# Layer-2 cross-attention: the reads of two tiles of keys together in every second step, with four buffers of exponentials

## The chip, the core and the metric

One NeuronCore of a Trainium2 chip runs the whole program, a four-layer block of attention and feed-forward parts in float32. The metric is the device time of one execution in microseconds (us). Three runs of the kernel before gave 1391.83, 1392.6 and 1385.4 us; their median is 1391.83 us.

## The reference, cut to what matters

The change touches one of the twelve parts, the cross-attention of layer 2. It has two batches of 128 queries and 32 heads of width 8. The queries attend to themselves (with a mask), and to a context of 2048 keys; both reads are summed, the second scaled by tanh of a gate for each head.

```python
q, k, v = heads(x @ Wq), heads(x @ Wk), heads(x @ Wv)      # 32 heads of 8
q, k = rope(q), rope(k)
w = softmax(max(q @ k.T * 8**-0.5 + mask, lowest))          # 128 x 128 for a head
out = w @ v
a_k, a_v = heads(context @ Wk), heads(context @ Wv)         # 2048 keys
out = out + tanh(gate) * softmax(q @ a_k.T * 8**-0.5) @ a_v
return out @ Wo
```

## The kernel before, in words

The function layer_L2X (from line 1509) writes out, engine by engine, a program of instructions that wait on semaphores. After a prologue (normalization, projections, rope), a loop runs over 6 stages. A stage is one batch and one of three groups of heads, c: groups 0 and 1 have 12 heads (three in each of four groups of 32 rows), group 2 has 8 (two in each). The order is (0,2), (0,0), (0,1), (1,0), (1,1), (1,2) as (batch, c); so stages 0 and 5 are of two heads and stages 1 to 4 of three. Each stage has 16 steps, one for each tile of 128 keys.

In step t of stage s TensorE issues, in this order:

- second_scores(s, t), line 1719: four matmuls, one for each group g of 32 rows, of keys by queries with the maximum already folded in; the result of each (128 keys by 384 or 256 columns) goes to its own PSUM bank. ScalarE takes the exponential of each bank into the buffer ex (line 1908).
- context_v, line 1651, in some steps: the values of two tiles of keys (in stage 0 at t = 5, in stage 2 at odd t from 3, in stage 3 at t = 1). ScalarE copies them (line 1835).
- first_scores for the next stage, line 1703: sets of four matmuls of 128 queries by 512 keys, each into its own bank, of which VectorE takes the row maximum (line 1996). At t % 4 == 1 there are two sets where the next stage has three heads, one where it has two; at t % 4 == 3 one set. Stage 5 issues none; the last step of a stage issues the first set for the stage after the next.
- self_scores, line 1665, at t % 4 == 3, taken by VectorE (line 1954).
- read(s, t - 1), line 1733: for each head the values of tile t - 1 (128 keys by 32 columns, as weights) times the exponentials, added up over the 16 tiles in one bank, "read". It waits until the exponentials of its tile are there. At t = 0 it is the last tile of the stage before.
- the other sets of first_scores; then self_read (line 1682, t % 4 == 0), context_k (line 1642, t % 4 == 1, stages 0 to 3), self_turn (line 1673, t % 4 == 2), turn_reads (lines 1689 and 1694, t = 2), turn_max (line 1711, t = 14).

All blocks but the read share a ring of seven PSUM banks. The class Turns hands them out in order: a take waits for the semaphore that says that the use seven takes back has been emptied by ScalarE or VectorE. A matmul of float32 is recorded as two instructions (two passes), so that the four matmuls of a block of scores count as x8.

The buffer ex holds the exponentials of NE = 3 tiles. Before the exponentials of step n, ScalarE waits for the read of tile n - NE. All engines work through their own list in order; TensorE's order is written out by hand in the loop.

Of the kernel before, what the change touches and what calls it, by code (L numbers as in the profile page):

```python
# [23 lines left out]
P = 128  # L24
B = 2
D = 256
# [3 lines left out]
NT = S2 // P  # L30
# [1478 lines left out]
def layer_L2X(env):  # L1509
# [5 lines left out]
    L = Layer(env, "L2X")  # L1515
# [3 lines left out]
    TRIO = 3 * P  # L1519
# [3 lines left out]
    ring = [L.bank(f"ring{j}") for j in range(NR)]  # L1523
    bank_o = L.bank("read")
    head = Head(L, ring[2])
    y = L.sb("y", [P, B, D])
    tail = Tail(L, y, ring[0], ring[1], w("Wo"))
    maskt = L.sb("mask", [P, B * TRIO])
    q, k = L.sb("q", [P, B, D]), L.sb("k", [P, B, D])
    tmp = L.sb("rope_tmp", [P, B, D])  # L1530
    kT = L.sb("self_kT", [P, NC, B, P])
    qm = L.sb("q_masked", [P, B, NC, 3, P])
    qx = L.sb("q_and_max", [P, 2, TRIO])
    mxs = L.sb("max_spread", [P, 2, 3, P])
    parts, mx = L.sb("max_parts", [P, 3, NG, 4]), L.sb("max", [P, 3 * NG])
    smx = L.sb("self_max", [P, 3])
    se, spT = L.sb("self_exp", [P, TRIO]), L.sb("self_probsT", [P, TRIO])
    soT = L.sb("self_readT", [P, NG, P])
    NE = 3
    ex = L.sb("context_exp", [P, NE, NG, TRIO])  # L1540
    qp, kp = ex[:, 0, 0:B, :], ex[:, 0, B:2 * B, :]
    cT = L.sb("context_kT", [P, 3, S2])
    cvp = L.sb("context_v_ones", [P, NT, NH * VW + 32 - VW])
    svp = L.sb("self_v_ones", [P, B, NH * VW + 32 - VW])
    cv, sv = (a[:, :, 0:NH * VW].rearrange("p t (h e) -> p t h e", e=VW) for a in (cvp, svp))
    oT = L.sb("readT", [P, TRIO])
    tg, inv, ya = L.sb("tanh_gate", [P, NH]), L.sb("inv_den", [P, 3 * NG]), L.sb("out_part", [P, 3 * NG * HD])
    names = ("dve_chain", "buffers_set", "mask_loaded", "gate_tanh", "qkv_done", "q_roped", "k_roped", "self_v_copied",
             "q_rope_ready", "k_rope_ready", "q_turned", "k_turned", "last_q_masked", "q_masked_ready", "self_kT_copied",
# [11 lines left out]
    NSTG = len(stages)  # L1561
# [3 lines left out]
    def heads(c):  # L1565
        return 2 if c == 2 else 3

    def head_at(c, g, j):
        return 12 * c + heads(c) * g + j

    def width(s):
        return heads(stages[s][1]) * P

    def done(n):

        return NG * n
# [8 lines left out]
    def first_sets(s, t):  # L1585

        x, n = t // 4, (sets[s + 1] // 4 if s + 1 < NSTG else 0)
        if t % 4 == 1:
            return [(s + 1, n * x + i) for i in range(1, n)]
        if t % 4 == 3 and x < 3 and n:  # L1590
            return [(s + 1, n * (x + 1))]
        if t == NT - 1 and s + 2 < NSTG:
            return [(s + 2, 0)]
        return []

    def v_tile(s, t):

        if s == 0 and t == 5:
            return 0, EARLY_V
        if s == 2 and t % 2 and t > 1:  # L1600
            return 1, (t - 3) // 2
        if s == 3 and t == 1:
            return 1, NT // 2 - 1
        return None
# [18 lines left out]
    def bank_of(sem, value):  # L1623
        return ring[at[sem.name, value]]

    with L.block() as block:
# [6 lines left out]
        def _(pe):  # L1633
# [12 lines left out]
            def context_v(b, j):  # L1646
                env.wait_context(pe, b, 2 * j // 4 * 4)
                bank = turns.take(pe, s_cvc, b * NT // 2 + j + 1)
                for u in range(2):
                    for kk in range(KC):  # L1650
                        i = nc.tensor.matmul(bank[:, u * D:(u + 1) * D], env.ctx(kk, b, 2 * j + u), wv[:, kk, :],
                                             start=(kk == 0), stop=(kk == KC - 1))
                i.then_inc(s_cv, 1)
# [7 lines left out]
            def self_scores(n):  # L1661
                (b, c), g = stages[n // NG], n % NG
                bank = turns.take(pe, s_st, n + 1)
                for j in range(heads(c)):
                    i = nc.tensor.matmul(bank[:, j * P:(j + 1) * P], qm[32 * g:32 * g + 32, b, c, j, :],
                                         kT[32 * g:32 * g + 32, c, b, :], start=True, stop=True)
                i.then_inc(s_ss, 1)
# [8 lines left out]
            def self_read(n):  # L1676
                (b, c), g = stages[n // NG], n % NG
                pe.wait_ge(s_spT, n + 1)
                bank = turns.take(pe, s_soc, n + 1)
                for j in range(heads(c)):  # L1680
                    h = head_at(c, g, j)
                    nc.tensor.matmul(bank[32 * j:32 * j + 32, 0:P], svp[:, b, h * VW:h * VW + 32],
                                     spT[:, j * P:(j + 1) * P], start=True, stop=True).then_inc(s_so, 1)
# [13 lines left out]
            def first_scores(s, i):  # L1697
                b, c = stages[s]
                blk, j = i // heads(c), i % heads(c)
                pe.wait_ge(s_ckc, 4 * s + blk + 1)  # L1700
                for g in range(NG):
                    bank = turns.take(pe, s_ft, before[s] + NG * i + g + 1)
                    nc.tensor.matmul(bank[:, :], qm[32 * g:32 * g + 32, b, c, j, :],  # L1703
                                     cT[32 * g:32 * g + 32, s % 3, blk * 512:(blk + 1) * 512],
                                     start=True, stop=True).then_inc(s_f, 1)

            def turn_max(s):
                pe.wait_ge(s_mx, s + 1)
                bank = turns.take(pe, s_qx, s + 1)
                for j in range(3):  # L1710
                    i = nc.tensor.transpose(bank[:, j * P:(j + 1) * P], mxs[:, s % 2, j, :], ident)
                i.then_inc(s_mt, 1)

            def second_scores(s, t):
                if t == 0:
                    pe.wait_ge(s_qx, s + 1)
                for g in range(NG):
                    bank = turns.take(pe, s_e, done(s * NT + t) + g + 1)
                    nc.tensor.matmul(bank[:, 0:width(s)], cT[32 * g:32 * g + 32, s % 3, t * P:(t + 1) * P],  # L1719
                                     qx[32 * g:32 * g + 32, s % 2, 0:width(s)], start=True, stop=True).then_inc(s_p, 1)  # L1720

            def read(s, t):
                b, c = stages[s]
                n = s * NT + t
                if t % 2 == 0:
                    pe.wait_ge(s_cvc, b * NT // 2 + t // 2 + 1)
                pe.wait_ge(s_e, done(n + 1))
                if t == 0 and s:
                    pe.wait_ge(s_oc, s)
                for j in range(heads(c)):  # L1730
                    for g in range(NG):
                        h = head_at(c, g, j)
                        i = nc.tensor.matmul(bank_o[32 * g:32 * g + 32, j * P:(j + 1) * P],  # L1733
                                             cvp[:, t, h * VW:h * VW + 32], ex[:, n % NE, g, j * P:(j + 1) * P],
                                             start=(t == 0 and j == 0), stop=(t == NT - 1), skip_group_check=True)
                        if j == heads(c) - 1:
                            i.then_inc(s_o, 1)
# [45 lines left out]
            for s in range(NSTG):  # L1783
                for t in range(NT):
                    n, r = NG * s + t // 4, t % 4
                    firsts = first_sets(s, t)
                    second_scores(s, t)
                    if v_tile(s, t):
                        context_v(*v_tile(s, t))
                    if firsts:  # L1790
                        first_scores(*firsts[0])
                    if r == 3 and n + 1 < NG * NSTG:
                        self_scores(n + 1)
                    if t:
                        read(s, t - 1)
                    elif s:
                        read(s - 1, NT - 1)
                    for f in firsts[1:]:
                        first_scores(*f)
                    if r == 0 and n:  # L1800
                        self_read(n - 1)
                    if r == 1 and s + 2 < NSTG:
                        context_k(s + 2, t // 4)
                    if r == 2:
                        self_turn(n)
                    if t == 2 and s:
                        turn_reads(s - 1)
                    if t == NT - 2 and s + 1 < NSTG:
                        turn_max(s + 1)
            read(NSTG - 1, NT - 1)  # L1810
            self_read(NG * NSTG - 1)
            turn_reads(NSTG - 1)
# [10 lines left out]
        def _(act):  # L1823
# [77 lines left out]
            for s in range(NSTG):  # L1901
                for t in range(NT):
                    n, m, r = s * NT + t, NG * s + t // 4, t % 4
                    if n >= NE:
                        act.wait_ge(s_o, done(n - NE + 1))
                    for g in range(NG):
                        act.wait_ge(s_p, done(n) + g + 1)
                        nc.scalar.activation(ex[:, n % NE, g, 0:width(s)], bank_of(s_e, done(n) + g + 1)[:, 0:width(s)], ACT.Exp,  # L1908
                                             scale=SCALE).then_inc(s_e, 1)
# [1485 lines left out]
```

## Time and profile before

| | |
|---|---|
| median of three runs | 1391.83 us |
| the profiled execution, its own time | 1388.13 us |
| its span | 1386.4 us |
| mean granted TensorE clock | 0.908 |
| TensorE matmul busy | 1119.1 us (81%) |
| VectorE busy | 691.6 us (50%) |
| ScalarE busy | 476.6 us (34%) |
| GpSimd busy | 156.1 us (11%) |
| the loop of 6 stages, about | 465 to 772 us of the span |

The profile page gives each engine's busy time over the whole span, a digit for each fortieth of it, the chain of work that ended last, and the costliest groups of instructions. PE is TensorE's matmul, PEld its weight load, DVE is VectorE, ACT ScalarE. Of a busy TensorE one must know that matmuls are pipelined and overlap: where it is busy all the time, the order in time (the timeline) shows how fast the blocks follow each other. In a timeline the first two numbers of a row are its start and its length in us; a row merges instructions of one line that follow each other, and xN is their number.

### The profile page before, as it was taken

What the parts mean: (1) busy time and instruction counts of PE and PEld (TensorE: products, weight loads), DVE (VectorE), ACT (ScalarE), POOL (GpSimd) and SP (SyncE); (2) the same over time, 40 slices, a digit from 0 to 9 for tenths busy, and PEclk for the clock granted to TensorE, in tenths of its full rate; (3) what the DMA queues carried; (4) which work ended last, traced back from release to release, by engine and by line L of the source; (5) the groups of instructions that cost most, each with busy time, mean ns of one, the idle gap of its engine ahead of it and who ended that gap; (6) DMA issues with size and microseconds to landing.
All of it is one profiled execution on the core that took longest, in us unless ns stands there. A gap on an engine that the chain in (4) does not pass through costs nothing. (4 is left out here: it accounts for less than half of the span.)

```text
span 1386.4 us, 24100 instructions
## 1 busy us (share of the span) xinstructions
PE 1119.1 (81%) x9813; PEld 771.5 (56%) x9813; DVE 691.6 (50%) x1741; ACT 476.6 (34%) x1027; POOL 156.1 (11%) x167
## 2 busy tenths in 40 slices
PE   6978889959859999999999776838555645676998
PEld 5856456637545555555566565615333324565886
DVE  4542456863337677656664342425454546364332
ACT  1101156743202355655567442303211212121322
POOL 0004000000001000000000000070444543000000
PEclk9988999989979999999999998968777777788999
DMA  8021200012012000000000101150333332003552
GB/s 352 1 91 46 107 1 2 2 54 95 1 43 103 1 2 1 2 2 1 2 2 2 74 1 55 37 164 13 92 92 92 103 97 75 0 14 152 188 198 79
DMA packets 16189, 84.55 MB, mean 61 GB/s; under 512 B 3152, under 2 KB 3664, under 8 KB 12368
## 3 DMA queue, kind: packets, MB, share of 16 engines
q1 hardware_dynamic: 7888, 57.84, 11.0%
q0 software_dynamic: 8192, 25.17, 6.5%
q8 instruction: 79, 1.29, 0.4%
q14 instruction: 30, 0.25, 0.1%
HBM read 82.74 MB, written 0.26 MB: 60 GB/s over the span
## 5 line engine op out<-in xcount | busy, mean ns | idle before, releaser
L1996 DVE TENSOR_REDUCE L2X_max_parts<-L2X_bank_ring 128x1 f32<-128x512 f32 x256 | 158.3, 683 | 87.3 <-PE L2X_bank_ring L1703 87.2
L1908 ACT ACTIVATE L2X_context_exp<-L2X_bank_ring 128x384 f32<-128x384 f32 (+1 forms) x384 | 144.2, 464 | 63.0 <-PE L2X_bank_ring L1719 60.3
L2327 POOL DMA_INDIRECT L2F_rows<-in_L2F_embed_dram,L2F_expert x128 | 123.4, 964 | 176.0 <-DVE L2F_acc L2490 101.4
L1703 PE MATMUL L2X_bank_ring<-L2X_context_kT,L2X_q_masked 32*128 32x512 f32 x512 | 98.1, 637 | 0.0
L976 ACT ACTIVATE L1X_probs<-L1X_clipped,L1X_drop,L1X_keep 128x1024 f32<-128x1024 f32 x64 | 77.6, 1237 | 32.3 <-DVE L1X_clipped L1034 25.0
L1034 DVE TENSOR_SCALAR L1X_clipped<-L1X_banks_scores 128x1024 f32<-128x1024 f32 x64 | 75.4, 1219 | 24.1 <-PE L1X_banks_scores L873 22.3
L1719 PE MATMUL L2X_bank_ring<-L2X_q_and_max,L2X_context_kT 32*128 32x384 f32 (+1 forms) x768 | 86.3, 498 | 0.0
L2372 ACT ACTIVATE L3X_k_features<-L2F_banks_pair 128x1024 f32<-128x1024 f32 x32 | 32.7, 1023 | 149.0 <-remote 115.0
L2269 PE MATMUL L2F_bank_sim<-L3X_k_features,L3X_v_ones 128*32 128x64 f32 x1024 | 36.7, 237 | 55.8 <-issue 55.7
L1733 PE MATMUL L2X_bank_read<-L2X_context_exp,L2X_context_v_ones 128*32 128x128 f32 x2048 | 76.3, 278 | 1.3 <-ACT L2X_context_exp L1908 1.0
L1733 PEld LDWEIGHTS L2X_bank_read<-L2X_context_exp,L2X_context_v_ones 128*32 128x32 f32 x2048 | 50.4, 110 | 44.8 <-issue 34.2
L2269 PEld LDWEIGHTS L2F_bank_sim<-L3X_k_features,L3X_v_ones 128*32 128x32 f32 x1024 | 24.3, 117 | 75.7 <-issue 70.0
L2490 DVE SCALAR_TENSOR_TENSOR L2F_acc<-L2F_rows,L2F_expert_weight,L2F_acc 128x256 f32<-128x256 f32 x128 | 62.2, 486 | 4.6
L2233 PE MATMUL L2F_bank_keys<-ctxT,slot 128*128 128x512 f32 x64 | 34.5, 666 | 36.0 <-ACT L3X_kT L2362 34.4
L2248 PE MATMUL L2F_banks_pair<-slot,L3X_kT 64*128 64x256 f32 x256 | 45.5, 456 | 15.3 <-issue 14.4
L1703 PEld LDWEIGHTS L2X_bank_ring<-L2X_context_kT,L2X_q_masked 32*128 32x128 f32 x512 | 41.8, 184 | 24.4 <-issue 12.4
L2485 DVE TENSOR_SCALAR L2F_z_exp<-L2F_z_exp 128x8 f32<-128x8 f32 x16 | 3.3, 204 | 101.1 <-ACT L2F_z_exp L2386 89.4
L1642 PE MATMUL L2X_bank_ring<-ctxT,slot 128*128 128x512 f32 x96 | 48.7, 631 | 2.1 <-PEq L178 2.1
L2259 PE MATMUL L2F_bank_sim<-slot,ctxT 128*128 128x272 f32 x128 | 42.9, 458 | 8.1 <-issue 8.1
L1719 PEld LDWEIGHTS L2X_bank_ring<-L2X_q_and_max,L2X_context_kT 32*128 32x128 f32 x768 | 32.9, 183 | 28.1 <-DVE L2X_max_parts L1996 13.8
L1827 ACT ACTIVATE L2X_context_kT<-L2X_bank_ring,consts 128x512 f32<-128x512 f32 x24 | 16.5, 689 | 74.1 <-PE L2X_bank_ring L1642 74.1
L873 PE MATMUL L1X_banks_scores<-L1X_q_blocks,L1X_kT 32*128 32x256 f32 x512 | 36.7, 400 | 6.1 <-DVE L1X_clipped L1034 5.3
(590 smaller groups left out, 2052.9 us busy)
## 6 DMA issues: line engine op xcount, KB each, us to landing
L3F_expert_weights<-in_L3F_experts_dram SPq DMA_DIRECT2D x16, 1280.0 KB, 5.6
L1A_groups<-in_L1A_groups_dram SPq DMA_DIRECT2D x3, 1536.0 KB, 9.9
ctxT<-in_ctxT_dram SPq DMA_DIRECT2D x8, 512.0 KB, 10.9
L0X_tokens<-in_L0X_tokens_dram SPq DMA_DIRECT2D x8, 512.0 KB, 15.5
slot<-in_L1A_dram SPq DMA_DIRECT2D x1, 3584.0 KB, 11.2
slot<-in_L0F_dram SPq DMA_DIRECT2D x1, 3072.0 KB, 10.4
slot<-in_L2A_dram SPq DMA_DIRECT2D x1, 3072.0 KB, 12.2
slot<-in_L2F_dram SPq DMA_DIRECT2D x1, 2476.5 KB, 8.9
```

What stands on the lines that cost most here:

```text
L976: nc.scalar.activation(pr[:, u % NP, :], sc[:, u % NP, :], ACT.Exp, bias=drop[:, n:n + 1], scale=keep[:, n:n + 1]).then_inc(s_p, 1)
L1034: nc.vector.tensor_scalar(sc[:, u % NP, :], pair_s[u % NPAIR][:, :], CLIP, -CLIP, ALU.min, ALU.max).then_inc(s_cl, 1)
L1642: i = nc.tensor.matmul(bank[:, :], wkp[:, kk, c * P:(c + 1) * P], env.ctx4(kk, b, blk), start=(kk == 0), stop=(kk == KC - 1))
L1703: nc.tensor.matmul(bank[:, :], qm[32 * g:32 * g + 32, b, c, j, :], cT[32 * g:32 * g + 32, s % 3, blk * 512:(blk + 1) * 512], start=True, s ...
L1719: nc.tensor.matmul(bank[:, 0:width(s)], cT[32 * g:32 * g + 32, s % 3, t * P:(t + 1) * P], qx[32 * g:32 * g + 32, s % 2, 0:width(s)], start ...
L1733: i = nc.tensor.matmul(bank_o[32 * g:32 * g + 32, j * P:(j + 1) * P], cvp[:, t, h * VW:h * VW + 32], ex[:, n % NE, g, j * P:(j + 1) * P], ...
L1908: nc.scalar.activation(ex[:, n % NE, g, 0:width(s)], bank_of(s_e, done(n) + g + 1)[:, 0:width(s)], ACT.Exp, scale=SCALE).then_inc(s_e, 1)
L1996: nc.vector.tensor_reduce(parts[:, j, g, blk:blk + 1], bank_of(s_ft, n)[:, :], AX, ALU.max).then_inc(s_ft, 1)
L2248: i = nc.tensor.matmul(pair[n % 2][:, at:at + 4 * FD], kT[lo:lo + 64, (n // 4) % 2, c, (t % 4) * P:(t % 4 + 1) * P], w3("Wkf")[lo:lo + 64, ...
L2269: i = nc.tensor.matmul(bank_kv[b][32 * ct:32 * ct + 32, i4 * FD:(i4 + 1) * FD], vo[:, n % NB, h * VW:h * VW + 32], kf[:, n % NB, r, c, ct ...
L2327: pool.indirect_dma_start(out=rows[:, n % NR, k, :], out_offset=None, in_=env.dram["L2F_embed"], in_offset=bass.IndirectOffsetOnAxis(idx[: ...
L2490: i = nc.vector.scalar_tensor_tensor(out=acc[:, b, :], in0=rows[:, n % NR, k, P:EMB], scalar=wt[:, n % 2, k:k + 1], in1=acc[:, b, :], op0= ...
```

## The change

In odd steps nothing is read any more. At an even t from 2 on, both read(s, t - 2) and read(s, t - 1) are issued, where read(s, t - 1) stood; at t = 0 of a later stage the two last tiles of the stage before; after the loop two reads, where there was one. The buffer of exponentials has four places (NE = 4). To make room for it in SBUF, three tiles lose their own storage: y lies on q, the self exponentials on k, and the tile readT on rope_tmp.

```diff
-    y = L.sb("y", [P, B, D])
+    q, k, tmp = (L.sb(n, [P, B, D]) for n in ("q", "k", "rope_tmp"))
+    y = q
     tail = Tail(L, y, ring[0], ring[1], w("Wo"))
     maskt = L.sb("mask", [P, B * TRIO])
-    q, k = L.sb("q", [P, B, D]), L.sb("k", [P, B, D])
-    tmp = L.sb("rope_tmp", [P, B, D])
...
-    se, spT = L.sb("self_exp", [P, TRIO]), L.sb("self_probsT", [P, TRIO])
+    se, spT = k[:, :, :].rearrange("p b d -> p (b d)")[:, 0:TRIO], L.sb("self_probsT", [P, TRIO])
     soT = L.sb("self_readT", [P, NG, P])
-    NE = 3
+    NE = 4
...
-    oT = L.sb("readT", [P, TRIO])
+    oT = tmp[:, :, :].rearrange("p b d -> p (b d)")[:, 0:TRIO]
...
                     if r == 3 and n + 1 < NG * NSTG:
                         self_scores(n + 1)
-                    if t:
+                    if t % 2 == 0 and t:
+                        read(s, t - 2)
                         read(s, t - 1)
-                    elif s:
+                    elif t == 0 and s:
+                        read(s - 1, NT - 2)
                         read(s - 1, NT - 1)
                     for f in firsts[1:]:
                         first_scores(*f)
...
+            read(NSTG - 1, NT - 2)
             read(NSTG - 1, NT - 1)
             self_read(NG * NSTG - 1)
             turn_reads(NSTG - 1)
```

## Rows read from the trace of the kernel before

**Rows 1.** The page, its head: the span.

```profile
span 1386.4 us, 24100 instructions
```

**Rows 2.** Busy time by stretch: stage 1; the first row names the columns.

```profile
core 0: us, PE busy (x) PEld busy (x) DVE busy (x) ACT busy (x) POOL busy (x), PEclk, DMA share, GB/s
...
517.30:574.60 57.30, 57.30 (x690) 32.93 (x687) 39.38 (x75) 32.84 (x81) 0.00 (x0) 1.00 0.01 2
```

**Rows 3.** The page, costliest groups: the reads; busy us, mean ns, idle before.

```profile
L1733 PE MATMUL L2X_bank_read<-L2X_context_exp,L2X_context_v_ones 128*32 128x128 f32 x2048 | 76.3, 278 | 1.3 <-ACT L2X_context_exp L1908 1.0
```

**Rows 4.** Timeline, TensorE, stage 1: start us, length us, then the block.

```profile
542.28 0.93 PE L1719 MATMUL L2X_bank_ring<-L2X_q_and_max,L2X_context_kT 32*128 32x384 f32 x8
...
545.86 0.60 PE L1719 MATMUL L2X_bank_ring<-L2X_q_and_max,L2X_context_kT 32*128 32x384 f32 x4
...
547.73 0.98 PE L1719 MATMUL L2X_bank_ring<-L2X_q_and_max,L2X_context_kT 32*128 32x384 f32 x8
548.48 1.92 PE L1703 MATMUL L2X_bank_ring<-L2X_context_kT,L2X_q_masked 32*128 32x512 f32 x8
550.32 0.86 PE L1733 MATMUL L2X_bank_read<-L2X_context_exp,L2X_context_v_ones 128*32 128x128 f32 x24
551.12 1.14 PE L1703 MATMUL L2X_bank_ring<-L2X_context_kT,L2X_q_masked 32*128 32x512 f32 x8
552.19 1.98 PE L1642 MATMUL L2X_bank_ring<-ctxT,slot 128*128 128x512 f32 x4
554.10 0.93 PE L1719 MATMUL L2X_bank_ring<-L2X_q_and_max,L2X_context_kT 32*128 32x384 f32 x8
...
556.23 0.93 PE L1719 MATMUL L2X_bank_ring<-L2X_q_and_max,L2X_context_kT 32*128 32x384 f32 x8
...
560.29 0.93 PE L1719 MATMUL L2X_bank_ring<-L2X_q_and_max,L2X_context_kT 32*128 32x384 f32 x8
561.14 0.86 PE L1733 MATMUL L2X_bank_read<-L2X_context_exp,L2X_context_v_ones 128*32 128x128 f32 x24
561.82 0.40 PE L1682 MATMUL L2X_bank_ring<-L2X_self_probsT,L2X_self_v_ones 128*32 128x128 f32 x6
```

**Rows 5.** Timeline of the same stretch, ScalarE, the weight load and VectorE; idle in brackets.

```profile
548.73 1.64 ACT L1908 ACTIVATE L2X_context_exp<-L2X_bank_ring 128x384 f32<-128x384 f32 x4
...
549.27 0.18 PEld L1703 LDWEIGHTS L2X_bank_ring<-L2X_context_kT,L2X_q_masked 32*128 32x128 f32 x1 [0.27 <-ACT L2X_context_exp L1908]
...
549.53 2.48 DVE L1996 TENSOR_REDUCE L2X_max_parts<-L2X_bank_ring 128x1 f32<-128x512 f32 x4 [1.11 <-PE L2X_bank_ring L1703]
...
558.03 2.48 DVE L1996 TENSOR_REDUCE L2X_max_parts<-L2X_bank_ring 128x1 f32<-128x512 f32 x4 [3.27 <-PE L2X_bank_ring L1703]
```

**Rows 6.** Timeline, stage 2, a step 3 with V between S and F.

```profile
602.88 0.93 PE L1719 MATMUL L2X_bank_ring<-L2X_q_and_max,L2X_context_kT 32*128 32x384 f32 x8
...
605.66 1.14 PE L1703 MATMUL L2X_bank_ring<-L2X_context_kT,L2X_q_masked 32*128 32x512 f32 x8
...
606.82 2.48 DVE L1996 TENSOR_REDUCE L2X_max_parts<-L2X_bank_ring 128x1 f32<-128x512 f32 x4 [4.91 <-PE L2X_bank_ring L1703]
...
608.18 0.93 PE L1719 MATMUL L2X_bank_ring<-L2X_q_and_max,L2X_context_kT 32*128 32x384 f32 x8
```

**Rows 7.** Timeline, stage 5, a step 1: two heads, no first scores.

```profile
753.82 0.77 PE L1719 MATMUL L2X_bank_ring<-L2X_q_and_max,L2X_context_kT 32*128 32x256 f32 x8
...
754.61 0.94 ACT L1908 ACTIVATE L2X_context_exp<-L2X_bank_ring 128x256 f32<-128x256 f32 x3
755.12 0.50 PE L1719 MATMUL L2X_bank_ring<-L2X_q_and_max,L2X_context_kT 32*128 32x256 f32 x4
```

**Rows 8.** Timeline, stage 0, a step 1: two heads, two sets of first scores.

```profile
494.41 0.83 PE L1719 MATMUL L2X_bank_ring<-L2X_q_and_max,L2X_context_kT 32*128 32x256 f32 x8
...
496.00 4.90 DVE L1996 TENSOR_REDUCE L2X_max_parts<-L2X_bank_ring 128x1 f32<-128x512 f32 x8 [0.41 <-PE L2X_bank_ring L1703]
...
498.33 1.98 PE L1642 MATMUL L2X_bank_ring<-ctxT,slot 128*128 128x512 f32 x4
```

## The prediction

> **What bounds the kernel now.** I read four views. First the page: the profiled execution spans 1386.4 us [rows 1]; its own time is 1388.13 us, so 1.7 us lie outside the span and the change touches none of them. Second, the busy time by stretch: the change lives in the loop over 6 stages of 16 steps, from about 465 to 772 us. In a stage of it TensorE is busy for the whole stretch (57.30 of 57.30 us) at a granted clock of 1.00, that is 2.4 GHz, while VectorE has 39.4 us and ScalarE 32.8 us of work [rows 2]. So TensorE is the engine whose program sets the end. The reader must not stop there: a matmul that waits for its bank doesn't show as idle beside others that are still in flight, so "100% busy" hides waits. Third, the page's group of the reads: 2048 matmuls, and only 1.3 us of idle time before them [rows 3]. The reads themselves wait for nothing; the exponentials are there when they come. The fourth buffer of exponentials can therefore give nothing by itself; it is only what makes the pairs legal. Fourth, the order in time on TensorE, beside ScalarE and VectorE [rows 4 to 8]. It shows two things that decide the case: where a change of tile shape costs time, and where a matmul stands waiting for one of the seven ring banks.
>
> Names for the walk: S second scores, F a set of first scores, R a read, K and V the projections of keys and values, q, t, r the self scores, turn and read. Before, four steps run: S R r | S F R F K | S R t | S F q R. After: S R R r | S F F K | S R R t | S F q. R takes no ring bank, so the order of the ring is unchanged: a block's matmul needs the bank of the take seven back.
>
> **Part 1, what is added at even steps.** The reads of the even tiles move from the odd steps to the next even one: 8 in each stage, 48 in all, of which the last (tile 14 of stage 5) stays where it was, at the end: 47 move, 32 of three heads and 15 of two. In an even step nothing is stalled: S to R takes 0.85 us (560.29 to 561.14), R to r, which has the same 128 x 32 shape, 0.68 us (561.14 to 561.82), against 0.80 us from R to a block of another shape (550.32 to 551.12) [rows 4]. Three heads are six passes of 128 columns, so a second read behind a first costs about 0.65 us, one of two heads two thirds, 0.44 us. Added: 32 x 0.65 + 15 x 0.44 = 27.4 us, with no cover: the row before and after it on TensorE are back to back.
>
> **Part 2, what is taken out at odd steps.** By TensorE's rows alone, each removed R takes 0.80 us with it (two heads 0.58, by the same passes), and one more change of shape: F to R or K takes 1.07 us (551.12 to 552.19), where two passes of 512 columns at 0.43 us would take 0.85, so 0.22 us. That would be 32 x 1.02 + 15 x 0.80 = 44.6 us, and the change would give 44.6 - 27.4 = 17 us. But R was also cover, because behind it come blocks that need banks which ScalarE and VectorE are still emptying. S at 547.73, the first exponential at 548.73; the load for the fourth F matmul is held until 549.27, released by that exponential [rows 5]. So S + 1.54 us is when the first of S's banks is back; the four exponentials are 0.38 us apart, which puts the fourth at S + 2.64. VectorE's maxima start 1.05 us after F (548.48 to 549.53) and run 0.60 us apart (2.48 us for 4, 4.90 for 8), each 0.68 long [rows 5, 8]. Now the walk, by kind of step.
>
> Step 1 (S F F K), three heads, no V: 8 of them. Before, K starts at 552.19 - 547.73 = 4.46. After, the second F's third matmul needs the fourth exponential (2.64), and its fourth the first maximum of the first F (549.53 + 0.68 = S + 2.48); start 2.70, two passes with their changes 1.07, K at 3.77. Saved 0.69 us of the 1.02: 5.5 us.
> Step 1 of stage 4, where no K follows and one F only: S is next, its third and fourth banks are the same two waits, so it is as if it began at 2.70, where the block behind the read now starts at 551.12 - 547.73 = 3.39. Saved 0.69, 4 of them: 2.8 us.
> Step 3 (S F q, then the next S), three heads, no V: 11 of them. Before, S to S is 4.06 us (556.23 to 560.29) where q shares the last F's rows of the array and 3.58 us otherwise (542.28 to 545.86) [rows 4]. After, the next S's fourth bank is that of the second F matmul: its maximum ends at 558.03 + 0.60 + 0.68 = 559.31, S + 3.08. So 3.13 us, saved 0.93 (3 times) and 0.45 (8 times): 6.3 us.
> Steps with V, in stage 2 above all: V takes 1.9 us between S and F, so that the exponentials are long back, and what is late is VectorE alone. F at 605.66, maxima from 606.82, the second ends at 608.10, and S stands at 608.18 already now [rows 6]. The read there is hidden to its last tenth: saved 0.0 in 4 steps 3. In the 5 steps 1 with V, the second F's fourth matmul waits for the first maximum (F + 1.84), where now it starts behind the read at F + 1.07 + 0.80 = 1.87: nothing saved either.
> Stage 0 (two heads): the maxima start at 496.00, so that the second F ends and K starts at 2.28 + 0.05 + 1.07 = 3.40 against 3.92 now (494.41 to 498.33) [rows 8]; two such steps, about 0.9 us for the first, which begins on a backlog, and 0.3 us over its steps 3: 2.2 us.
> Stage 5 (two heads, no F): S after S waits for the first exponential of the step. S 753.82, exponential 754.61; three of them take 0.94 us and start 0.28 apart, so one ends at S + 1.17, against 1.30 us now (753.82 to 755.12) [rows 7]: saved some 0.15 in 7 steps, 1.0 us.
> Sum: 5.5 + 2.8 + 6.3 + 0 + 2.2 + 1.0 = 17.8 us, of 44.6 that TensorE's rows alone would give.
>
> **The fourth buffer and the shared storage** (y on q, self exponentials on k, readT on rope_tmp): the old owners are last read in the prologue, before the loop; no wait is added, and the rows show nothing that depends on an address. Below, the fourth buffer could give the 1.3 us of rows 3; above, a move of storage can't be priced from a row, and I take 0 for both.
>
> **Sum:** +27.4 - 17.8 = +9.6 us, on 1388.13 gives 1397.7. The median of the runs shown, 1391.83, lies 3.7 us above that execution; on it the sum gives 1401.4. I forecast 1400.
>
> The Trainium skill, "TensorEngine Tiling (Array Packing)", Key Properties, says that changing the tiling mode drains TensorE. The trace agrees, at 0.1 us on either side of a block [rows 4]; that rule alone is the rival of 17 us below. The same page, PSUM Bottleneck, warns that tiling speeds up TensorE but not the emptying of PSUM; that speaks against this change, and rows 5 and 6 agree: the block behind the removed read is released by ScalarE or VectorE.
>
> **Rivals.**
> A. The changes of shape decide, and the ring has slack that I don't see (matmuls held up would let the others through, and the engines that empty the banks would gain on TensorE in the longer even steps). Then 17 us are gained: 1391.83 - 17 = 1375. For it: each of the 94 changes is real time. Against: the held load and the S at 608.18 sit within 0.1 us of their releases. It decides only if banks come back at least 0.6 us earlier relative to their step than now. Chance 0.08.
> B. Gains and costs nearly cancel: TensorE's separate row groups let three of four matmuls of S or F run ahead, and the late one overlaps with them and with what follows by some 0.2 us more than I allow, in the some 35 odd steps that save anything: -7 us, +3 us in all, 1395. Chance 0.17.
> C. A second read behind a first doesn't go at the pace of R before r but at the full 0.80 us (both add into the same bank): 47 x 0.15 = 7 us more, +17 us, 1408. Against it: R's own three heads also add into that bank and run at 0.11 us a pass. Chance 0.08.
>
> **How the numbers follow.** The forecast has 0.67, with its own range of 1395 to 1405: the steps without V could each be off by 0.1 us (4 us), and the base is known to 4 us. 0.5% is 7 us here, about what a measurement of this kernel can tell from no change. +9.6 is 2.6 above that bound, so of the forecast's 0.67 I put 0.48 beyond it and 0.19 within; B is within for 0.14 and faster for 0.01, slower for 0.02; C slower; A faster. Slower 0.58, same 0.33, faster 0.09. The range runs from 1389, which takes most of B, to 1407, which stops short of C and leaves A out.
>
> **What would show it right or wrong.** Right: S to S over an even step grows by 0.65 us (two heads 0.44); K behind S F F at S + 3.8; in stage 2 no odd step gets shorter, so that this stage alone grows by 4 us or more; loads for F and S held by ScalarE's exponentials and VectorE's maxima. Wrong: odd steps shorter by about 1.0 us each (A), a second R of 0.80 us (C), or a loop that got longer in steps that this walk leaves alone. What happens outside 465 to 772 us should be the same to a few tenths.

## The result: half a per cent slower, and the profile after

The kernel after takes 1398.31 us (median of 20 runs, 1391.75 to 1408.33), the kernel before 1390.2 us (median of 20, 1381.54 to 1396.55). The ratio is 1.0053, 95% interval [1.0034, 1.0072]: 7.4 us slower by the ratio (the medians themselves lie 8.1 us apart), where +9.6 was forecast.

The span of the profiled execution is 1392.3 us, 5.9 us more than in [rows 1]. Spans scatter by some us in code that is the same in both, so the loop is better measured by itself: from the start of the first exponential to the start of the last, which one row gives (the instructions that write the tile of exponentials: count, ns at least, median and at most, first and last start). The kernel before:

```profile
L1908 ACT ACTIVATE L2X_context_exp<-L2X_bank_ring x384: 378/490/557, 466.3 to 770.9; 128x384 f32<-128x384 f32 x128, 128x256 f32<-128x256 f32 x64
```

The kernel after:

```profile
L1910 ACT ACTIVATE L2X_context_exp<-L2X_bank_ring x384: 378/490/519, 469.1 to 781.6; 128x384 f32<-128x384 f32 x128, 128x256 f32<-128x256 f32 x64
```

That is 304.6 and 312.5 us: the loop got 7.9 us longer, and what lies outside it is not longer. (The expectations below count to the end of the last exponential, 0.4 us more: 304.9 and 312.8.) The first exponentials of each stage cut it into stages: stage 0 went from 51.9 to 52.1, stage 1 from 57.3 to 57.2, stage 2 from 67.9 to 71.6, stage 3 from 58.7 to 60.0, stage 4 from 43.9 to 44.5, and stage 5 (to the start of its last exponential) from 24.8 to 27.1 us. Nearly half of it, 3.7 us, came in stage 2, the one with the projections of values in its odd steps; the prediction wanted 4 us or more there.

The timeline of TensorE in stage 1 after, over the steps 3, 0, 1 and 2, is what answers to [rows 4]. The line numbers of the blocks are smaller by one here; the tile L2X_k under the turn holds the self exponentials.

```profile
546.33 0.93 PE L1718 MATMUL L2X_bank_ring<-L2X_q_and_max,L2X_context_kT 32*128 32x384 f32 x8
547.08 1.49 PE L1702 MATMUL L2X_bank_ring<-L2X_context_kT,L2X_q_masked 32*128 32x512 f32 x7
...
549.02 1.36 PE L1718 MATMUL L2X_bank_ring<-L2X_q_and_max,L2X_context_kT 32*128 32x384 f32 x7
550.31 1.52 PE L1732 MATMUL L2X_bank_read<-L2X_context_exp,L2X_context_v_ones 128*32 128x128 f32 x48
551.65 0.40 PE L1681 MATMUL L2X_bank_ring<-L2X_self_probsT,L2X_self_v_ones 128*32 128x128 f32 x6
551.97 0.93 PE L1718 MATMUL L2X_bank_ring<-L2X_q_and_max,L2X_context_kT 32*128 32x384 f32 x8
552.72 3.07 PE L1702 MATMUL L2X_bank_ring<-L2X_context_kT,L2X_q_masked 32*128 32x512 f32 x16
555.73 1.98 PE L1641 MATMUL L2X_bank_ring<-ctxT,slot 128*128 128x512 f32 x4
557.64 0.93 PE L1718 MATMUL L2X_bank_ring<-L2X_q_and_max,L2X_context_kT 32*128 32x384 f32 x8
558.50 1.52 PE L1732 MATMUL L2X_bank_read<-L2X_context_exp,L2X_context_v_ones 128*32 128x128 f32 x48
559.95 0.55 PE L1672 MATMUL L2X_bank_ring<-consts,L2X_k 128*128 128x128 f32 x3
560.42 0.93 PE L1718 MATMUL L2X_bank_ring<-L2X_q_and_max,L2X_context_kT 32*128 32x384 f32 x8
```

Read it by starts. A step 3 is read together with the scores behind it: in the new order the first matmuls of the next S start early, and its last ones wait, so the start of the read behind that S is what counts. The pair of reads takes 1.34 us up to the self read (550.31 to 551.65), against 0.68 for one; an even step grew by 0.66 us (S at 557.64 to S at 560.42 is 2.78, where [rows 4] have 2.13). In step 1, K stands at 555.73 - 551.97 = 3.76 us after S, against 4.46; the walk said 3.77. In step 3, the read behind the next S stands 3.98 us after S (546.33 to 550.31); the walk said 3.13 + 0.85. The sixteen F instructions take 3.07 us, where 16 passes of four in parallel would be 1.7: the rest is waiting, while "busy" counts on.

The weight loads of the same stretch name who is waited for (idle in brackets; after):

```profile
552.40 0.52 PEld L1702 LDWEIGHTS L2X_bank_ring<-L2X_context_kT,L2X_q_masked 32*128 32x128 f32 x6
553.52 0.29 PEld L1702 LDWEIGHTS L2X_bank_ring<-L2X_context_kT,L2X_q_masked 32*128 32x128 f32 x2 [0.60 <-ACT L2X_context_exp L1910]
```

And over the whole loop, the loads of S and F, before and then after (busy us, mean ns, idle us before them and what ended it):

```profile
L1703 PEld LDWEIGHTS L2X_bank_ring<-L2X_context_kT,L2X_q_masked 32*128 32x128 f32 x440 | 38.6, 185 | 19.1 <-issue 8.2 <-ACT L2X_context_exp L1908 6.6 <-DVE L2X_out_part L1980 0.5
L1719 PEld LDWEIGHTS L2X_bank_ring<-L2X_q_and_max,L2X_context_kT 32*128 32x128 f32 x764 | 32.5, 183 | 28.1 <-DVE L2X_max_parts L1996 13.8 <-issue 11.7 <-ACT L2X_context_exp L1908 2.7
```

```profile
L1718 PEld LDWEIGHTS L2X_bank_ring<-L2X_q_and_max,L2X_context_kT 32*128 32x128 f32 x764 | 48.0, 183 | 30.6 <-DVE L2X_max_parts L1998 17.8 <-issue 7.5 <-ACT L2X_context_exp L1910 3.4
L1702 PEld LDWEIGHTS L2X_bank_ring<-L2X_context_kT,L2X_q_masked 32*128 32x128 f32 x440 | 42.0, 188 | 30.3 <-ACT L2X_context_exp L1910 14.2 <-issue 5.6 <-DVE L2X_max_parts L1998 3.7
```

The idle time that ScalarE's exponentials end before F's loads went from 6.6 to 14.2 us, and that which VectorE's maxima end, before both, from 13.8 to 21.5 us.

Stage 2 after, a step 3 with V, answers to [rows 6]; first TensorE, then VectorE:

```profile
607.99 0.93 PE L1718 MATMUL L2X_bank_ring<-L2X_q_and_max,L2X_context_kT 32*128 32x384 f32 x8
...
612.40 1.78 PE L1718 MATMUL L2X_bank_ring<-L2X_q_and_max,L2X_context_kT 32*128 32x384 f32 x6
614.11 1.52 PE L1732 MATMUL L2X_bank_read<-L2X_context_exp,L2X_context_v_ones 128*32 128x128 f32 x48
615.44 0.39 PE L1681 MATMUL L2X_bank_ring<-L2X_self_probsT,L2X_self_v_ones 128*32 128x128 f32 x6
```

```profile
611.93 2.48 DVE L1998 TENSOR_REDUCE L2X_max_parts<-L2X_bank_ring 128x1 f32<-128x512 f32 x4 [5.56 <-PE L2X_bank_ring L1702]
```

The second maximum ends at 611.93 + 0.60 + 0.68 = 613.21, and the pair starts 0.90 us later, at 614.11; from S to a read it takes 0.85 us in [rows 4], where S waits for nothing. From S to the read behind the next S it is 6.12 us, before 608.18 + 0.86 - 602.88 = 6.16: the read was taken out and nothing came back.

### The profile page after: what moved, and what is told of

Read it like the earlier page. It is cut to its first block and busy times, and to the rows that moved or that the text cites. A ratio compares the mean times of both kernels' runs of the same rounds, so it can differ in the third digit from the quotient of the medians.

```text
span 1392.3 us, 24099 instructions
## 1 busy us (share of the span) xinstructions
PE 1140.9 (82%) x9813; PEld 792.3 (57%) x9813; DVE 691.4 (50%) x1741; ACT 482.0 (35%) x1027; POOL 156.5 (11%) x167
## 5 line engine op out<-in xcount | busy, mean ns | idle before, releaser
L1718 PE MATMUL L2X_bank_ring<-L2X_q_and_max,L2X_context_kT 32*128 32x384 f32 (+1 forms) x768 | 108.9, 497 | 0.2
L1702 PE MATMUL L2X_bank_ring<-L2X_context_kT,L2X_q_masked 32*128 32x512 f32 x512 | 101.2, 630 | 0.0
L2250 PE MATMUL L2F_banks_pair<-slot,L3X_kT 64*128 64x256 f32 x256 | 51.3, 461 | 22.9 <-issue 21.4
L1732 PE MATMUL L2X_bank_read<-L2X_context_exp,L2X_context_v_ones 128*32 128x128 f32 x2048 | 66.1, 275 | 0.8 <-ACT L2X_context_exp L1910 0.8
L1718 PEld LDWEIGHTS L2X_bank_ring<-L2X_q_and_max,L2X_context_kT 32*128 32x128 f32 x768 | 48.4, 183 | 30.6 <-DVE L2X_max_parts L1998 17.8
L1702 PEld LDWEIGHTS L2X_bank_ring<-L2X_context_kT,L2X_q_masked 32*128 32x128 f32 x512 | 45.2, 187 | 35.6 <-ACT L2X_context_exp L1910 14.2
L2250 PEld LDWEIGHTS L2F_banks_pair<-slot,L3X_kT 64*128 64x128 f32 x256 | 29.0, 216 | 36.0 <-issue 32.3
```

The costliest lines, as they stand in the source:

```text
L2250: i = nc.tensor.matmul(pair[n % 2][:, at:at + 4 * FD], kT[lo:lo + 64, (n // 4) % 2, c, (t % 4) * P:(t % 4 + 1) * P], w3("Wkf")[lo:lo + 64, ...
```

## The experiments

All loops are from the first start to the last start of the row above, in each kernel's own profile. Each is from one profiled execution. Stages that an edit doesn't touch repeat closely: with the storage alone changed, the six stages are within 0.25 us of those before.

**The storage alone, and the two halves of the move.** The edits, each on the kernel after:

```diff
 # e1_buffers_only
-                    if t % 2 == 0 and t:
-                        read(s, t - 2)
+                    if t:
                         read(s, t - 1)
-                    elif t == 0 and s:
-                        read(s - 1, NT - 2)
+                    elif s:
                         read(s - 1, NT - 1)
...
-            read(NSTG - 1, NT - 2)
             read(NSTG - 1, NT - 1)
 # e2_step1_moved: only the reads of t % 4 == 1 go to the next step
-                    if t % 2 == 0 and t:
+                    if t % 4 == 2:
                         read(s, t - 2)
+                    if t and t % 4 != 1:
                         read(s, t - 1)
                     elif t == 0 and s:
-                        read(s - 1, NT - 2)
                         read(s - 1, NT - 1)
...
-            read(NSTG - 1, NT - 2)
             read(NSTG - 1, NT - 1)
 # e3_step3_moved: only those of t % 4 == 3
-                    if t % 2 == 0 and t:
+                    if t and t % 4 == 0:
                         read(s, t - 2)
+                    elif t == 0 and s:
+                        read(s - 1, NT - 2)
+                    if t and t % 4 != 3:
                         read(s, t - 1)
                     elif t == 0 and s:
-                        read(s - 1, NT - 2)
                         read(s - 1, NT - 1)
```

> The four buffers and the shared storage of the change, with the reads in their old places (one in every step). Both parts of the sum were put at 0. Theory of the prediction: the loop of the six stages stays at 304.9 us (within 0.5 us) and the time at that of the kernel before. Rival: a part of the 7.9 us by which the loop got longer is due to where the tiles now lie, or to a wait on the storage; then the loop is 1 us longer or more here already.

> Only the reads of the steps t % 4 == 1 are moved, to the next step; those of t % 4 == 3 stay. 24 reads move: 16 of three heads at 0.65 us, 8 of two at 0.44, 13.9 us added. Saved by the walk: 8 x 0.69 + 4 x 0.69 + 1.9 (stage 0) + 0.6 (stage 5), nothing in the five steps with V: 10.8 us. Theory: the loop is 3.1 us longer than before (308.0). If the changes of tile shape alone decided: 24 x 0.36 = 8.6 us shorter (296.3). If a second read cost 0.80 us: 3.6 us more than the theory.

> Only the reads of the steps t % 4 == 3 are moved, to the next step; those of t % 4 == 1 stay. 23 reads move: 16 x 0.65 + 7 x 0.44 = 13.5 us added. Saved by the walk: 6.3 us in 11 steps of three heads, 0.3 in stage 0, 0.4 in stage 5, nothing in the four steps of stage 2 (VectorE's second maximum): 7.0 us. Theory: the loop is 6.5 us longer than before (311.4), of which 2.6 in stage 2. This and the run that moves the others should add up to the whole change. If the changes of shape alone decided: 23 x 0.36 = 8.3 us shorter.

The rows of the three, in this order:

```profile
L1907 ACT ACTIVATE L2X_context_exp<-L2X_bank_ring x384: 377/491/572, 474.8 to 779.2; 128x384 f32<-128x384 f32 x128, 128x256 f32<-128x256 f32 x64
```

```profile
L1909 ACT ACTIVATE L2X_context_exp<-L2X_bank_ring x384: 378/490/557, 472.4 to 779.8; 128x384 f32<-128x384 f32 x128, 128x256 f32<-128x256 f32 x64
```

```profile
L1912 ACT ACTIVATE L2X_context_exp<-L2X_bank_ring x384: 378/490/578, 475.3 to 784.7; 128x384 f32<-128x384 f32 x128, 128x256 f32<-128x256 f32 x64
```

Loops of 304.4, 307.4 and 309.4 us, that is -0.2, +2.8 and +4.8 us. The times: 1389.74, 1393.31 and 1396.82 us beside 1390.43 before, ratios 1.0007 [0.9977, 1.0037], 1.0043 [1.0006, 1.0081] and 1.0033 [0.9998, 1.0068]; the ratios of the two halves can't be told apart, the loops can. Storage and fourth buffer cost and give nothing. The halves add up to 7.6 of the 7.9 us. The first half was +3.1 by the walk, the second +6.5: its miss of 1.7 us is as large as that of the whole sum. By the starts of the exponentials, more than half of it lies where a stage ends: step 15 and the next step 0 together were to grow by 0.2 us (three heads, no V) and grew by 0.04; behind stage 2 they were to grow by 0.65 and grew by 0.47 (0.58 with the step behind them). There the old order had a wait already (that step 0 was 2.02 us long, not 1.86), which the walk of one group of four steps did not have. Some 0.3 us more lie in stage 0, where steps 11 and 12 together grew by 0.05 us: that step 11 was 3.30 us long against 2.85 for the steps 3 and 7, as the longer steps 11 of three heads were (4.06 against 3.58), and the walk had priced these in the stages of three heads only.

**What a read is worth where it stood.** The reads of one step in two are left out of the old order, with the waits that count them; the sums then lack half of the keys. The edit for the even tiles (for the odd ones the same with 0):

```diff
             def read(s, t):
+                if t % 2 != 1:
+                    return
...
-                    if n >= NE:
-                        act.wait_ge(s_o, done(n - NE + 1))
+                    if n >= NE and (n - NE) % 2 == 1:
+                        act.wait_ge(s_o, NG * ((n - NE) // 2 + 1))
```

> The old order; the reads of the even tiles, those of the odd steps, are left out altogether (48 reads and their changes of tile shape; the sums then lack half of the keys). It measures by itself what an odd step gives back when its read is gone. Theory (the read was cover for banks that ScalarE and VectorE still hold): the loop gets 17.8 us shorter, to 287.1, and in stage 2 no step with V gets shorter. Rival (TensorE's rows alone): 44.6 us shorter, to 260.

> The complement: the reads of the odd tiles, those of the even steps, are left out, the others stay. TensorE's rows alone: 24 steps 0 at 0.65 us or 0.44, 24 steps 2 at 0.80 or 0.58 give 31 us, the loop at 274. Theory: the even steps were without a stall, but a step of bare scores runs into ScalarE's four exponentials (2.64 us from one S to the release of its last bank), so that much less comes back: 5 to 15 us, the loop between 290 and 300.

```profile
L1909 ACT ACTIVATE L2X_context_exp<-L2X_bank_ring x384: 377/491/516, 467.6 to 753.2; 128x384 f32<-128x384 f32 x128, 128x256 f32<-128x256 f32 x64
```

```profile
L1909 ACT ACTIVATE L2X_context_exp<-L2X_bank_ring x384: 377/491/572, 472.0 to 764.3; 128x384 f32<-128x384 f32 x128, 128x256 f32<-128x256 f32 x64
```

Loops of 285.6 and 292.3 us. The reads of the odd steps gave back 19.0 us, where the walk had 17.8 and TensorE's rows alone 44.6. Stage 2 as a whole gave 1.6 us, and half of that is its step 1 without V (6.4 to 5.7 us); with V, steps 3 and 4 together kept their length within 0.05 us. This is the direct measure of the disputed term. The complement gave back 12.3 us of 31: a single read in an even step is worth little too, since without it the next F waits for ScalarE (by the starts of S in stage 1, steps 4 and 6 got 0.64 and 0.79 us shorter, and the steps 5 and 7 behind them 0.40 and 0.61 longer). By these numbers both stand in slots that are more than half waiting time. (Ratios 0.9893 [0.9764, 1.0022] and 0.9881 [0.9727, 1.0034].)

**Banks that come back earlier.** Both orders with maxima over 128 of 512 columns, then with exponentials over 128 columns as well. The reads then take the first head's exponentials for all heads:

```diff
-nc.vector.tensor_reduce(parts[:, j, g, blk:blk + 1], bank_of(s_ft, n)[:, :], AX, ALU.max).then_inc(s_ft, 1)
+nc.vector.tensor_reduce(parts[:, j, g, blk:blk + 1], bank_of(s_ft, n)[:, 0:P], AX, ALU.max).then_inc(s_ft, 1)
 # the second pair of kernels has these edits too; the lines are cut at their right end
-nc.scalar.activation(ex[:, n % NE, g, 0:width(s)], bank_of(s_e, done(n) + g + 1)[:, 0:width(s)], ACT.Exp,
+nc.scalar.activation(ex[:, n % NE, g, 0:P], bank_of(s_e, done(n) + g + 1)[:, 0:P], ACT.Exp,
-cvp[:, t, h * VW:h * VW + 32], ex[:, n % NE, g, j * P:(j + 1) * P],
+cvp[:, t, h * VW:h * VW + 32], ex[:, n % NE, g, 0:P],
```

> The old order of reads, but VectorE takes the maxima of the first scores over 128 columns of each bank in place of 512 (the maximum is then not that of all keys; this is left out), so that its banks come back some 0.4 us earlier each and 1.6 us earlier for a set. It is the base for the same cut in the new order. In the old order the reads stand where the wait would be, so little is won: the loop should be 0 to 4 us shorter than 304.9.

> The new order with the same maxima over 128 columns. Theory (what the removed read leaves behind is a wait for VectorE's maxima and ScalarE's exponentials): steps 3 now save 1.0 us (15 of them), the five steps 1 with V also 1.0, the others 0.69 as before, stage 0 4.4 us, stage 5 1.0: 33 us saved against 27 added. The loop should be about 6 us shorter than its twin in the old order, where the unchanged kernels differ by 7.9 us the other way. If VectorE's maxima are not what ends the wait, the two still differ by +7.9 us.

> The old order, with the maxima over 128 columns and the exponentials over 128 columns of each bank (the heads 2 and 3 of a group are left out; all reads use the first head's exponentials, so that TensorE's work is the same). Base for its twin in the new order. The holds of 0.8 us on the fourth first-score matmul become shorter by some 0.2 to 0.3 us (exponential 0.49 to 0.25 long), in 30 steps: the loop some 5 to 10 us shorter than 304.9.

> The new order with maxima and exponentials over 128 columns. Theory: with both releases short, the second first-score set and the next step's scores hardly wait behind what the read used to cover, so that the gain comes near what TensorE's own rows give, 17 us: the loop 12 to 17 us shorter than its twin in the old order. If something else than ScalarE and VectorE holds TensorE, the twins differ as the whole kernels do, by +7.9 us.

The rows, maxima alone (old order, new order), then both:

```profile
L1908 ACT ACTIVATE L2X_context_exp<-L2X_bank_ring x384: 377/491/550, 465.9 to 767.3; 128x384 f32<-128x384 f32 x128, 128x256 f32<-128x256 f32 x64
```

```profile
L1910 ACT ACTIVATE L2X_context_exp<-L2X_bank_ring x384: 377/491/517, 472.0 to 769.2; 128x384 f32<-128x384 f32 x128, 128x256 f32<-128x256 f32 x64
```

```profile
L1908 ACT ACTIVATE L2X_context_exp<-L2X_bank_ring x384: 271/279/325, 472.2 to 763.9; 128x128 f32<-128x128 f32 x192
```

```profile
L1910 ACT ACTIVATE L2X_context_exp<-L2X_bank_ring x384: 272/279/341, 471.5 to 757.0; 128x128 f32<-128x128 f32 x192
```

Loops of 301.4 and 297.2 us: with shorter maxima alone the pairs win by 4.2 us, where they lose 7.9 with whole ones. So the sign of the change hangs on VectorE's release of the banks, as the theory says. The old order gained 3.2 us, nearly all of it in stage 0 (49.0 against 51.9 us), its other stages nothing. For the pairs the forecast was 6: in a step 1 with V the new order won 0.4 us of the 1.0 (7.25 against 7.68), because a maximum can't begin before its own matmul's two passes are done, 1.15 us after its start (the same rows show it: F at 604.48, first maximum at 605.63), however short it is.

```profile
604.48 1.14 PE L1702 MATMUL L2X_bank_ring<-L2X_context_kT,L2X_q_masked 32*128 32x512 f32 x8
605.63 0.88 DVE L1998 TENSOR_REDUCE L2X_max_parts<-L2X_bank_ring 128x1 f32<-128x128 f32 x4 [8.24 <-PE L2X_bank_ring L1702]
```

With both cut, 291.7 and 285.5 us, the pairs win 6.2. I had expected 12 to 17, and of the old order alone a gain of 5 to 10 us, where it gained 12.9. In single steps the theory holds to the full. Here are S and K of step 5 of stage 1 (S F F K), in the old order and in the new one:

```profile
534.46 0.93 PE L1719 MATMUL L2X_bank_ring<-L2X_q_and_max,L2X_context_kT 32*128 32x384 f32 x8
538.71 1.98 PE L1642 MATMUL L2X_bank_ring<-ctxT,slot 128*128 128x512 f32 x4
```

```profile
531.83 0.93 PE L1718 MATMUL L2X_bank_ring<-L2X_q_and_max,L2X_context_kT 32*128 32x384 f32 x8
535.07 1.98 PE L1641 MATMUL L2X_bank_ring<-ctxT,slot 128*128 128x512 f32 x4
```

K stands 4.25 us after S with the read between them and 3.24 without it: 1.01 us came back, of the 1.02 that TensorE's rows give a read with its changes of shape, where the whole kernels gave 0.70. For the sum the forecast was too high. Stage 2 got only 0.2 us shorter by the pairs, and stage 5 got 2.3 us longer. I had treated the release as ScalarE's and VectorE's time alone. A large part of it is TensorE's own: 1.0 us from S to its first exponential, 1.05 to 1.15 from F to its first maximum. A faster ScalarE or VectorE takes away only the rest. That this is all that is left in stages 2 and 5 was not tried by itself. (The times of these four are 1288.62, 1283.29, 1286.5 and 1276.14 us, beside 1298.82 us for the kernel before on the same chip; ratios 0.9931 [0.9903, 0.9959], 0.988 [0.9809, 0.9951], 0.9905 [0.9876, 0.9933] and 0.9825 [0.9786, 0.9864].)

**One bank less.**

```diff
-    NR = 7
+    NR = 6
```

> The old order with a ring of six banks in place of seven. Each block then waits for the use six back, in step 1 and 3 the second exponential (0.38 us later), with V the third maximum (0.6 us later). Theory: 30 holds longer by 0.4 us and 9 by 0.6: the loop some 15 to 19 us longer, 320 to 324. If the ring isn't what holds TensorE: no change.

> The new order with six banks. Theory: behind S F q the next scores wait for the third maximum in place of the second (0.6 us against 0.4 in the old order), the rest as in the twin: 18 to 22 us longer than the new order with seven banks (312.8), at 331 to 335, so the twins differ by 10 to 12 us in place of 7.9. If changes of shape decide, the difference stays or shrinks.

```profile
L1908 ACT ACTIVATE L2X_context_exp<-L2X_bank_ring x384: 378/490/558, 477.0 to 799.6; 128x384 f32<-128x384 f32 x128, 128x256 f32<-128x256 f32 x64
```

```profile
L1910 ACT ACTIVATE L2X_context_exp<-L2X_bank_ring x384: 377/491/510, 468.4 to 803.4; 128x384 f32<-128x384 f32 x128, 128x256 f32<-128x256 f32 x64
```

Loops of 322.6 and 335.0 us: +18.0 in the old order (15 to 19 expected) and +22.5 in the new one (18 to 22, so just above). One bank is worth 18 us with the same instructions, and the pairs now lose 12.4 us instead of 7.9 (10 to 12 expected). Ratios 1.0131 [0.9993, 1.0269] and 1.02 [1.0039, 1.0361]. Together with the shorter maxima this moves the difference both ways by the one thing that the theory names.

No version beats both kernels by what can be measured: by the stages of the run that moved the reads of step 1 alone, the pairs gain only in stages 1 and 4, 0.23 us each. An eighth bank wasn't tried; the eighth is the one the reads add up in.

## Why the prediction was right, by its steps

- Part 1, +27.4 us. The pace of a second read was 0.66 us of 0.65 (three heads). Even steps t % 4 == 2 grew from 2.13 to 2.78. Rival C (0.80 us) is out.
- Part 2, the cut of 44.6 us to 17.8. What the two halves of the sum leave is 27.4 - 7.9 = 19.5 us given back; left out altogether, the reads gave 19.0. Step 1 without V: K at 3.76 of 3.77. Step 3: 3.98 of 3.98. Step 3 of stage 2: 0.04 us came back, of 0.0 forecast; its steps 1 with V 0.02 to 0.05. One sign was set too high: stage 2 was to grow by 4 us or more and grew by 3.7.
- In stage 5, by the starts of the exponentials, steps 1 saved next to nothing (1.38 before and after, 0.15 forecast), but the step 2 behind each grew by 0.23 us and not by 0.44, which makes up for it.
- The fourth buffer and the storage: 0 forecast, -0.2 us measured.
- Rival A (the changes of shape decide, -17 us) is out: in the run with half of the reads left out not even the reads' own time came back (19.0 us, where 0.80 us for a read of three heads and 0.58 for one of two give 34.9), and the same move gains or loses by how long VectorE holds the banks. The changes of shape do cost their 0.1 us on either side: where the banks come back early, 1.01 us of 1.02 is given back. That fits the drain at a change of tiling mode that the Trainium skill states ("TensorEngine Tiling (Array Packing)", Key Properties). In the whole kernels they were not what ended last.
- Rival B (some 0.2 us more overlap in each odd step, -7 us): the sum did come out less, but by 1.7 us. Of the +9.6 us, +7.9 came in the loop, and 7.4 to 8.1 in the time. The missing 1.7 us lie in the 17.8 of part 2, mostly where stages meet, and not in overlap within a step: in the steps of three heads inside a stage the walk is met within 0.1 us.
- The time: 1398.31, forecast 1400. On the 20 runs of the kernel before (1390.2), +9.6 would have given 1399.8. That the base of the forecast, taken between 1388.13 and 1391.83, met these runs to 0.2 us was luck; it was known to 4 us. The sign is clear of the interval; whether the change passes 0.5% is not, since 1.0053 has an interval from 1.0034 to 1.0072.

## What to carry to other kernels

Before moving work to save TensorE's changes of shape, write down for every block behind it which bank it takes and who empties that one when. A block that looks like pure cost may stand exactly in the time in which the next one would wait, and then its place is the cheap one: here 48 reads cost 19.0 us in all where they stood, and 19.0 + 7.9 = 26.9 where they went. TensorE's busy time doesn't show such waits; the idle time before its weight loads shows a part of them (15.3 us more after the change, where some 25 of the 44.6 us did not come back).

## What the runs showed of the hardware that I had not expected

The first bank of a block of scores comes back late mostly because of TensorE itself: with four row groups side by side the first reader starts 1.0 us (384 columns) to 1.15 us (512 columns) after the block, and then holds the bank for 0.5 us (exponential) or 0.68 us (maximum). For the fourth bank it is the reader's queue: four exponentials take 1.64 of the 2.64 us. A cut of the maxima from 2.48 us for four to 0.88 left the steps of the old order as long as they were from stage 1 on.

On one chip every program ran 7% faster (1298.82 us for the kernel before there, 1390 to 1397 elsewhere); these are the runs with shorter maxima and exponentials. The loop is not where that comes from: with short maxima on that chip its stages 1 to 5 have the same lengths as in the kernel before elsewhere, within 0.1 us. The difference is outside, in the layer-2 feed-forward part, where GpSimd issues 128 indirect gathers. Its idle time before them, before (first) and in the run with short maxima in the old order (second):

```profile
L2327 POOL DMA_INDIRECT L2F_rows<-in_L2F_embed_dram,L2F_expert x128 | 123.4, 964 | 176.0 <-DVE L2F_acc L2490 101.4 <-DVE L2F_expert L2458 37.5 <-issue 37.0
```

```profile
L2327 POOL DMA_INDIRECT L2F_rows<-in_L2F_embed_dram,L2F_expert x128 | 125.9, 983 | 86.5 <-issue 38.4 <-DVE L2F_expert L2458 37.3 <-DVE L2F_acc L2490 10.8
```

The 90 us are waits for buffers that VectorE frees (101.4 against 10.8 us). VectorE need not be where they begin, though. Between the gathers TensorE itself crawls where the kernel is slower. Its weight loads of one line (L2248), while GpSimd issues gathers, before and then in the run with short maxima:

```profile
918.20 0.28 PEld L2248 LDWEIGHTS L2F_banks_pair<-slot,L3X_kT 64*128 64x128 f32 x1 [1.81 <-issue]
920.33 0.28 PEld L2248 LDWEIGHTS L2F_banks_pair<-slot,L3X_kT 64*128 64x128 f32 x1 [1.84 <-issue]
```

```profile
908.46 0.73 PEld L2248 LDWEIGHTS L2F_banks_pair<-slot,L3X_kT 64*128 64x128 f32 x8
```

Eight loads go out in 0.73 us in one case, and one in some 2 us in the other, with idle time that the profile gives to no other engine ("issue"). What slows TensorE there stays open.
